# Cross attention and ternary FFN on one core: queries by tokens, four pairs of heads in flight, unrolled engine orders

## The chip, the cores and the metric

The kernel runs on one core of a Trainium2 chip. The metric is the device time of one execution in microseconds (us), lower is better. A core has five engines that take their instructions in order and meet only through semaphores: PE (matrix multiply; PEld is its weight load), DVE, ACT, POOL, and SP, which here only issues DMAs. The profile is a hardware trace of one execution.

## The reference, cut to what matters

```python
# x (4, 256, 256), ctx (4, 256, 128), 16 heads of 128, 1024 hidden
def xattn(h, ctx, Wq, Wk, Wv, Wo, gq, gk):
    q = rmsnorm((h @ Wq).reshape(B, Sq, H, D), gq)      # x * rsqrt(mean(x^2) + 1e-5) * g
    k = rmsnorm((ctx @ Wk).reshape(B, Skv, H, D), gk)
    v = (ctx @ Wv).reshape(B, Skv, H, D)
    attn = softmax(einsum('bqhd,bkhd->bhqk', q, k) / sqrt(D))
    return einsum('bhqk,bkhd->bqhd', attn, v).reshape(B, Sq, H * D) @ Wo
x = x + xattn(layernorm(x), ctx, ...)
w1, w2 = ternary(W_fc), ternary(W_proj)                 # groups of 64: round(w / mean|w|), times mean|w|
h = square(relu(layernorm(x) @ w1.T))
x = x + rms_norm(h) @ w2.T
```

## The kernel before, in words

The attention is done in 32 steps: 4 batches times 8 pairs of heads. One step takes one pair of heads of one batch through the whole chain, and the steps overlap. Matrices that need more than one fp32r pass are split into a high part (names with h at the end: qh, kh, PTh, Oh, Wqh) and a low part (ql, kl, PTl, Ol, Wql), and each product is three matmuls of 256 columns: `three` emits them at L547, L548 and L549. High parts are ACT copies out of PSUM, low parts DVE subtractions; Wqh, Wql, Wkh and Wkl are made by POOL from the raw loads. Wv is folded into Wo at the start (WWh, WWl), so attention multiplies the probabilities with the raw context (ch, cl) in bank bO, and project adds Oh and Ol times WW into bank bY.

Queries come out of PE transposed (bank bA, features on partitions). Their squares (qsq, ACT) are summed over the features by four matmuls against a column of ones (`sums_q`, L621), DVE adds the epsilon (qv), POOL takes the power -1/2 (fq, L297), and fq enters later, as the scale of the exponential and in the bias nb (DVE L918, maximum times fq). Keys come out by tokens (bank bB): ACT squares, DVE sums (L883), POOL takes the power (kv L291, rk L293), DVE multiplies (kn L887), and PE transposes kn. After exp (L416, accumulating the sums su) DVE takes the reciprocal rs; the probabilities of head 0 are normalised by POOL (L308), those of head 1 by ACT (L424). PE transposes them (L585).

The ternary weights of the FFN are prepared beside attention, a 32nd part in each step: ACT converts 2 groups (L429) and sums their absolute values (L433), DVE compares (L938, L939: wpos, wneg), POOL subtracts and scales (L314, L317, written into Wor's space).

The order on each engine is written out by hand in its `body(i)`, with hardware loops (Fori) over most steps. Each step has queries of pair i+1, keys of i+2, scores of i+1 and attention of i. After the steps comes the FFN (`up`, `down`, `square`, `hidden`), which the change leaves as it is, apart from the ramp into it.

Of the kernel before, what the change touches and what calls it, by code (L numbers as in the profile page):

```python
# [5 lines left out]
def xattn_ffn(nc, x, ctx, Wq, Wk, Wv, Wo, gq, gk, W_fc, W_proj, out):  # L6

# [18 lines left out]
    P = 128  # L26
# [17 lines left out]
    SG = NG // STEPS  # L44
# [10 lines left out]
    with es:  # L55
# [3 lines left out]
        def sem(name):  # L59
# [5 lines left out]
        Wqr = sb("Wqr", [P, KC, 2, D])  # L65
        Wkr = sb("Wkr", [P, 2, D])
# [4 lines left out]
        gg = sb("gg", [P, 1])  # L71
        fpr = sb("fpr", [P, NG, GROUP])
# [10 lines left out]
        xn = sb("xn", [P, NT, DIM])  # L83

# [12 lines left out]
        wabs = sb("wabs", [P, SG, GROUP], bf16)  # L97
        gsum = sb("gsum", [P, NG])
        gsr = sb("gsr", [P, SG], bf16)
        wpos = sb("wpos", [P, SG, GROUP], bf16)  # L100
        wneg = sb("wneg", [P, SG, GROUP], bf16)
# [40 lines left out]
        yo = xn  # L142

# [981 lines left out]
```

## Time and profile before

| | |
|---|---|
| runs | 370.31, 370.45, 375.02 us (median 370.45) |
| span of the profiled execution, first to last instruction | 373.6 us |
| time of the profiled execution around its span | not listed apart; its span is 3.15 us above the median of the runs |
| PE, PEld busy | 347.3 us (93%), 330.7 us (89%) |
| DVE, ACT, POOL busy | 308.3 us (83%), 295.5 us (79%), 256.4 us (69%) |
| granted TensorE clock, mean | 0.981 |

Read it by stage: the opening (0 to about 40 us), 32 steps that repeat (about 40 to 320 us), and the FFN (to 373.6 us). Matmuls overlap in the records: one of 256 columns lasts 0.28 us and the next starts 0.12 us later, so the cost of a matmul is the spacing of starts. The same holds for ACT and DVE, whose records overlap by some 0.1 us.

### The profile page before, as it was taken

The numbers are of one execution on the slowest core, as the hardware profiler recorded it, in microseconds if no ns is written. First come the engines' busy times: TensorE is split into PE (matmuls) and PEld (weight loads), VectorE is DVE, ScalarE is ACT, GpSimd is POOL, SyncE is SP. The second block draws the span as 40 slices with busy tenths as digits, with TensorE's granted clock in tenths as the row PEclk, the third lists the DMA queues.
The fourth block names the chain that finished last, engine by engine and source line by source line (L and its number), as shares of the span: only waits on it lengthen the run. The fifth ranks groups of instructions, "written<-read, shape, count | busy, mean of one in ns | idle before, by whom it ended". The sixth has DMA issues, their size and how long they took to land.

```text
span 373.6 us, 9069 instructions
## 1 busy us (share of the span) xinstructions
PE 347.3 (93%) x2720; PEld 330.7 (89%) x2720; DVE 308.3 (83%) x697; ACT 295.5 (79%) x810; POOL 256.4 (69%) x386
## 2 busy tenths in 40 slices
PE   6778999999999999999999999999999999888975
PEld 5768999999999999999999999999999998767865
DVE  2797788888888888888888898888888986799991
ACT  3447888888888888888888888888888888777750
POOL 3653777777777787777777877777778773065761
PEclk9989999999999999999999999999999999999995
DMA  6980111111111111111111111111111100000012
GB/s 212 366 281 6 55 42 42 42 42 42 44 44 42 42 42 45 42 42 44 42 44 43 42 43 42 44 42 44 45 51 53 51 1 0 2 0 2 0 38 75
DMA packets 20341, 20.72 MB, mean 55 GB/s; under 512 B 1504, under 2 KB 19936, under 8 KB 20192
## 3 DMA queue, kind: packets, MB, share of 16 engines
q1 hardware_dynamic: 20032, 20.45, 16.9%
q8 instruction: 12, 0.20, 0.2%
q14 instruction: 9, 0.07, 0.1%
q10 hardware_dynamic: 288, 0.00, 0.0%
HBM read 19.40 MB, written 1.05 MB: 55 GB/s over the span
## 4 chain that ended last, share of the span: by engine, by line
PE 48%; DVE 17%; POOL 13%; issue 12%; DMA 4%; ACT 3%; POOLq 1%; SPq 0%; DVEq 0%; ACTq 0%
POOL fq L297 7%; PE bY L547 6%; DVE WWl L869 4%; PE bT L585 4%; PE bY L549 4%; PE bY L548 4%; PE bA L547 3%; PE bA L548 3%; PE bA L549 3%; PE bT L595 3%; POOL Wkh L274 3%; DVE Ol L869 3%; DMA Wkr<-in_L_xattn_Wk 3%; PE bO L547 2%; PE bO L549 2%
## 5 line engine op out<-in xcount | busy, mean ns | idle before, releaser
L416 ACT ACTIVATE Pr<-bS,nb,fq 128x256 f32<-128x256 f32 x128 | 70.9, 564 | 1.7 <-DVE nb L918 1.7
L411 ACT ACTIVATE Oh<-bO 128x256 fp32r<-128x256 f32 x64 | 24.6, 385 | 29.5 <-PE bO L549 29.1
L277 POOL TENSOR_TENSOR Wql<-Wqr,Wqh 128x512 fp32r<-128x512 f32 x32 | 41.4, 1293 | 5.9 <-POOL Wqh L274 5.9
L914 DVE TENSOR_REDUCE mx<-bS 128x2 f32<-128x512 f32 x64 | 43.8, 684 | 1.0 <-PE bS L549 0.6
L547 PE MATMUL bY<-WWh,Oh 128*128 (+1 forms) x128 | 39.1, 305 | 5.8 <-DVE Ol L869 4.9
L869 DVE TENSOR_TENSOR PTl<-bT,PTh 128x512 fp32r<-128x512 f32 x64 | 43.5, 681 | 0.9 <-ACT PTh L403 0.5
L547 PE MATMUL bS<-kh,qh 128*128 128x256 f32 x128 | 41.5, 324 | 0.6 <-DVE kl L900 0.6
L869 DVE TENSOR_TENSOR ql<-bA,qh 128x512 fp32r<-128x512 f32 x32 | 22.1, 691 | 22.1 <-ACT qh L399 22.1
L403 ACT ACTIVATE PTh<-bT 128x512 fp32r<-128x512 f32 x64 | 38.0, 594 | 1.6
L585 PE MATMUL bT<-ident,Pr 128*128 128x128 f32 x256 | 38.4, 273 | 0.4 <-ACT Pr L424 0.4
L297 POOL TENSOR_TENSOR fq<-qv,mhalf 128x4 f32<-128x4 f32 x32 | 32.5, 1014 | 7.3 <-DVE qv L910 6.9
L274 POOL TENSOR_SCALAR Wkh<-Wkr 128x256 fp32r<-128x256 f32 x32 | 12.9, 404 | 35.6 <-PE bB L549 31.5
L547 PE MATMUL bO<-PTh,ch 128*128 128x256 f32 x128 | 36.3, 284 | 0.5 <-DVE PTl L869 0.5
L547 PE MATMUL bA<-xTh,Wqh 128*128 128x256 f32 x128 | 36.8, 287 | 0.0
L548 PE MATMUL bA<-xTl,Wqh 128*128 128x256 f32 x128 | 36.6, 286 | 0.0
L308 POOL TENSOR_SCALAR Pr<-Pr,rs 128x256 f32<-128x256 f32 x64 | 30.1, 481 | 9.3 <-DVE rs L923 6.3
L549 PE MATMUL bA<-xTh,Wql 128*128 128x256 f32 x128 | 36.3, 283 | 0.0
L549 PE MATMUL bS<-kh,ql 128*128 128x256 f32 x128 | 36.0, 281 | 0.0
L548 PE MATMUL bS<-kl,qh 128*128 128x256 f32 x128 | 36.0, 281 | 0.0
L549 PE MATMUL bO<-PTh,cl 128*128 128x256 f32 x128 | 35.9, 281 | 0.0
L549 PE MATMUL bY<-WWh,Ol 128*128 (+1 forms) x128 | 35.8, 279 | 0.0
L548 PE MATMUL bY<-WWl,Oh 128*128 (+1 forms) x128 | 35.8, 279 | 0.0
(172 smaller groups left out, 1293.0 us busy)
## 6 DMA issues: line engine op xcount, KB each, us to landing
Wqr<-in_L_xattn_Wq SPq DMA_DIRECT2D x32, 256.0 KB, 2.5
Wkr<-in_L_xattn_Wk SPq DMA_DIRECT2D x32, 128.0 KB, 2.4
Wor<-in_L_xattn_Wo SPq DMA_DIRECT2D x2, 1024.0 KB, 9.6
Wvr<-in_L_xattn_Wv SPq DMA_DIRECT2D x1, 1024.0 KB, 9.6
fpr<-in_L_ffn_W_fc SPq DMA_DIRECT2D x1, 1024.0 KB, 11.2
fpr<-in_L_ffn_W_proj SPq DMA_DIRECT2D x1, 1024.0 KB, 12.8
out<-xn SPq DMA_DIRECT2D x4, 256.0 KB, 2.2
xt<-in_x SPq DMA_DIRECT2D x1, 768.0 KB, 7.5
```

The source lines that it names most:

```text
L277: gp.tensor_tensor(lo, src, hi.bitcast(f32), ALU.subtract).then_inc(done, 1)
L297: gp.tensor_tensor(fq[:, :], qv[:, :], mhalf[:, 0:UT], ALU.pow).then_inc(fq_done, 1)
L308: last = gp.tensor_scalar(Pr[0][:, t, :], Pr[0][:, t, :], rs[0][:, t:t + 1], 1.0, ALU.mult, ALU.mult)
L403: act.activation(PTh[u][:, :, :].rearrange(flat3), bT[u][:, :], ACT.Copy).then_inc(pth_done[u], 1)
L411: act.activation(Oh[u][:, :], bO[:, u * SQ:(u + 1) * SQ], ACT.Copy).then_inc(oh_done, 1)
L416: last = act.activation(Pr[u][:, t, :], bS[u][:, t * SKV:(t + 1) * SKV], ACT.Exp, bias=nb[u][:, t:t + 1], scale=fq[:, QT * u + t:QT * u + ...
L547: pe.matmul(dst, sth, mvh, start=start, stop=False, **kw)
L548: pe.matmul(dst, sth, mvl, start=False, stop=False, **kw)
L549: return pe.matmul(dst, stl, mvh, start=False, stop=stop, **kw)
L585: last = pe.transpose(bT[u][:, k * SQ + t * P:k * SQ + (t + 1) * P], Pr[u][:, t, k * P:(k + 1) * P], ident[:, :])
L869: return dve.tensor_tensor(dst, src, hi.bitcast(f32), ALU.subtract)
L914: dve.tensor_reduce(mx[u][:, :], bS[u][:, :].rearrange("p (t k) -> p t k", t=QT), AX.X, ALU.max).then_inc(mx_done[u], 1)
```

## The change

Queries are now computed by tokens (x as the stationary operand, Wq moving), as keys were, with the same number of matmuls. ACT squares and accumulates the sums of the eight 128-column pieces of queries and keys directly out of PSUM (`square_q`, `square_k`: 8 instructions in place of 2). POOL's `norms` adds the epsilon and takes the power of all 8 columns in one call. DVE multiplies queries and keys out of PSUM (qn, kn), PE transposes both, and high and low parts are taken from the transposed banks (queries in bT0, keys in bT1, banks they share with the probabilities). `sums_q`, qv, fq, mx and DVE's sum of ksq are gone; the exponential has a constant scale, and nb is the negated maximum, written by one reduction. Both heads' probabilities are normalised by POOL. The ternary work goes in 8 chunks of 8 groups (128x512), one every third pass: the sums of absolute values are a DVE reduction (L948), no ACT instructions. Raw weights have two buffers. All loops are unrolled into one sequence on each engine, with queries of pair i+2, keys of i+2 (i+3 on ACT and POOL), scores of i+1, attention and projection of i-1 in PE's pass i. The opening, its banks (two instead of four for WW; one bank, bY, for the transposed x of batches 1 to 3) and the load order are new; semaphores are renamed.

The core of the diff:

```diff
-            def rsqrt_q(n):
-                gp.wait_ge(qv_done, n + 1)
-                gp.tensor_tensor(fq[:, :], qv[:, :], mhalf[:, 0:UT], ALU.pow).then_inc(fq_done, 1)
+            def norms(n):
+                gp.wait_ge(sqk_done, n + 1)
+                gp.wait_ge(sqq_done, n + 1)
+                gp.tensor_scalar(sse[:, :], ss[:, :], EPS * D, None, ALU.add).then_inc(sse_done, 1)
+                gp.wait_ge(sse_done, n + 1)
...
+                gp.tensor_tensor(rr[:, :], sse[:, :], mhalf[:, 0:2 * UT], ALU.pow).then_inc(r_done, 1)
...
+            for i in range(-2, STEPS):
+                if pair(i + 3):
                     split_k(i + 3)
...
+                if pair(i):
+                    norm_p(i, 1)
+                if pair(i + 2):
+                    norms(i + 2)
+                if pair(i + 3):
+                    split_q(i + 3)
+                if i == -1:
+                    ln_rstd(2, 1, B - 1)
+                if pair(i + 1):
+                    norm_p(i + 1, 0)
+                if i >= 4 and (i - 4) % 3 == 0 and (i - 4) // 3 < CHUNKS:
+                    ternary((i - 4) // 3)
...
+            def square_q(n):
                 act.wait_ge(q_done, n + 1)
-                act.activation(qsq[:, :, :].rearrange(flat3), bA[:, :], ACT.Square).then_inc(qsq_done, 1)
-                act.activation(qh[:, :, :].rearrange(flat3), bA[:, :], ACT.Copy).then_inc(qh_done, 1)
...
+                for j in range(UT):
+                    last = act.activation(sqj[:, j, :], bA[:, j * D:(j + 1) * D], ACT.Square,
+                                          accum_out=ss[:, j:j + 1])
+                last.then_inc(sqq_done, 1)
```

ACT's and PE's sequence after the change (the lines for the opening left out):

```python
for i in range(-2, STEPS + 1):              # ACT
    o_hi(i - 1, 1); square_q(i + 2); p_hi(i, 0); exps(i + 1, 0); p_hi(i, 1); exps(i + 1, 1)
    o_hi(i, 0); q_hi(i + 2); k_hi(i + 2); square_k(i + 3)
    if i >= 1 and (i - 1) % 3 == 0 and (i - 1) // 3 < CHUNKS:
        ternary((i - 1) // 3)
for i in range(-1, STEPS):                  # PE
    attend(i - 1, 0); turn_q(i + 1); keys(i + 2); turn_k(i + 1); queries(i + 2); attend(i - 1, 1)
    turn_p(i, 0); scores(i + 1, 0); scores(i + 1, 1); project(i - 1, 1); project(i - 1, 0); turn_p(i, 1)
for i in range(-3, STEPS):                  # DVE
    o_lo(i, 1); maxes(i + 2, 0); maxes(i + 2, 1); p_lo(i + 1, 0); q_norm(i + 3); k_norm(i + 3)
    recip(i + 2, 0); p_lo(i + 1, 1); o_lo(i + 1, 0); q_lo(i + 3); recip(i + 2, 1); k_lo(i + 3)
    if i >= 2 and (i - 2) % 3 == 0 and (i - 2) // 3 < CHUNKS:
        t_scale((i - 2) // 3)
    if i >= 3 and (i - 3) % 3 == 0 and (i - 3) // 3 < CHUNKS:
        t_compare((i - 3) // 3)
```

Two places in the order, before and after. The numbers behind names are banks and heads. **The ternary work and what stands behind it.** POOL before, one pass of its loop (the pass runs in a circle):

```order
L274 TENSOR_SCALAR Wkh<-Wkr 128x256
L277 TENSOR_TENSOR Wkl<-Wkr,Wkh 128x256
L297 TENSOR_TENSOR fq<-qv,mhalf 128x4
L274 TENSOR_SCALAR Wqh<-Wqr 128x512
L277 TENSOR_TENSOR Wql<-Wqr,Wqh 128x512
L291 TENSOR_SCALAR kv<-ssk 128x4
L293 TENSOR_TENSOR rk<-kv,mhalf 128x4
L308 TENSOR_SCALAR Pr0<-Pr0,rs0 128x256 x2
L314 TENSOR_TENSOR wpos<-wpos,wneg 128x128
L317 TENSOR_TENSOR Wor<-wpos,gsr 128x128
```

POOL now, from `norms(6)` in its pass i = 4 to `norms(7)` in pass 5:

```order
L327 TENSOR_SCALAR sse<-ss 128x8
L332 TENSOR_TENSOR rr<-sse,mhalf 128x8
L319 TENSOR_SCALAR Wqh<-Wqr1 128x512
L321 TENSOR_TENSOR Wql<-Wqr1,Wqh 128x512
L337 TENSOR_SCALAR Pr0<-Pr0,rs0 128x256 x2
L345 TENSOR_TENSOR wpos<-wpos,wneg 128x512
L347 TENSOR_TENSOR Wor<-wpos,gsr 128x512
L308 TENSOR_SCALAR Wkh<-Wkr0 128x256
L310 TENSOR_TENSOR Wkl<-Wkr0,Wkh 128x256
L337 TENSOR_SCALAR Pr1<-Pr1,rs1 128x256 x2
L327 TENSOR_SCALAR sse<-ss 128x8
L332 TENSOR_TENSOR rr<-sse,mhalf 128x8
```

The two separate powers became one of 8 columns, head 1's normalisation came in, and a ternary chunk of four times the size stands, in every third pass, ahead of the next norms. On DVE, before, a step from head 1's maxima to the keys' product:

```order
L914 TENSOR_REDUCE mx1<-bS1 128x2
L918 SCALAR_TENSOR_TENSOR nb1<-mx1,fq 128x2
L929 TENSOR_SCALAR gsr<-gsum 128x2
L923 RECIPROCAL rs0<-su0 128x2
L938 TENSOR_TENSOR wpos<-Wvr,gsr 128x128
L939 SCALAR_TENSOR_TENSOR wneg<-Wvr,gsr 128x128
L869 TENSOR_TENSOR Ol1<-bO,Oh1 128x256
L887 TENSOR_TENSOR kn<-bB,rk 128x512
```

DVE now, its pass i = 3, from the products of pair 6 to the first chunk's comparison:

```order
L907 TENSOR_TENSOR qn<-bA,rr 128x512
L913 TENSOR_TENSOR kn<-bB,rr 128x512
L935 RECIPROCAL rs0<-su0 128x2
L892 TENSOR_TENSOR PTl1<-bT1,PTh1 128x512
L892 TENSOR_TENSOR Ol0<-bO,Oh0 128x256
L892 TENSOR_TENSOR ql<-bT0,qh 128x512
L935 RECIPROCAL rs1<-su1 128x2
L922 SCALAR_TENSOR_TENSOR kl<-bT1,gg,kh 128x512
L958 TENSOR_TENSOR wpos<-Wvr,gsr 128x512
L959 SCALAR_TENSOR_TENSOR wneg<-Wvr,gsr 128x512
```

The comparison moved from among the waits for exp to behind the low part of the keys, which itself needs the transposed keys. **The squares.** ACT before, from Oh of head 1 into the next step:

```order
L411 ACTIVATE Oh1<-bO 128x256
L416 ACTIVATE Pr1,su1<-bS1,nb1,fq 128x256 x2
L490 REGISTER_ALU
L490 COMPARE_AND_BRANCH
L398 ACTIVATE qsq<-bA 128x512
```

ACT now:

```order
L410 ACTIVATE sqj,ss<-bB 128x128 x4
L452 ACTIVATE Oh1<-bO 128x256
L419 ACTIVATE sqj,ss<-bA 128x128 x4
L446 ACTIVATE PTh0<-bT0 128x512
L438 ACTIVATE Pr0,su0<-bS0,nb0 128x256 x2
```

The four accumulating squares of the queries stand directly behind Oh of head 1, the exponentials behind them.

## Rows read from the trace of the kernel before

**Rows 1.** Timeline of PE, one step: start, us, line, operation, out<-in, [idle before].

```profile
181.97 0.60 PE L585 MATMUL bT<-ident,Pr 128*128 128x128 f32 x4
...
182.53 0.28 PE L548 MATMUL bB<-Wkl,cTh 128*128 128x256 f32 x1
182.65 0.28 PE L549 MATMUL bB<-Wkh,cTl 128*128 128x256 f32 x1
...
183.12 0.95 PE L621 MATMUL bA<-ones,qsq 128*128 128x1 f32 x8
...
188.51 0.28 PE L549 MATMUL bO<-PTh,cl 128*128 128x256 f32 x1
```

**Rows 2.** Timeline of ACT, the same step.

```profile
182.17 0.69 ACT L407 ACTIVATE kh<-bT,gg 128x512 fp32r<-128x512 f32 x1
...
185.02 0.26 ACT L433 ACTIVATE wabs<-Wvr 128x64 bf16 x1
...
188.83 0.39 ACT L411 ACTIVATE Oh<-bO 128x256 fp32r<-128x256 f32 x1 [0.70 <-PE bO L549]
189.11 0.56 ACT L416 ACTIVATE Pr<-bS,nb,fq 128x256 f32<-128x256 f32 x1
```

**Rows 3.** Timeline of POOL: one row of the opening, then one step.

```profile
14.04 1.33 POOL L302 TENSOR_TENSOR rstd<-lnv,mhalf 128x6 f32<-128x6 f32 x1 [3.08 <-DVE lnv L854]
...
189.54 0.94 POOL L308 TENSOR_SCALAR Pr<-Pr,rs 128x256 f32<-128x256 f32 x2
190.44 0.43 POOL L314 TENSOR_TENSOR wpos<-wpos,wneg 128x128 bf16<-128x128 bf16 x1
191.05 0.40 POOL L317 TENSOR_TENSOR Wor<-wpos,gsr 128x128 bf16<-128x128 bf16 x1 [0.18 <-POOL wpos L314]
192.72 0.40 POOL L274 TENSOR_SCALAR Wkh<-Wkr 128x256 fp32r<-128x256 f32 x1 [1.27 <-PE bB L549]
...
194.01 1.01 POOL L297 TENSOR_TENSOR fq<-qv,mhalf 128x4 f32<-128x4 f32 x1
195.01 0.62 POOL L274 TENSOR_SCALAR Wqh<-Wqr 128x512 fp32r<-128x512 f32 x1
...
197.18 0.19 POOL L291 TENSOR_SCALAR kv<-ssk 128x4 f32<-128x4 f32 x1
197.46 1.02 POOL L293 TENSOR_TENSOR rk<-kv,mhalf 128x4 f32<-128x4 f32 x1
```

**Rows 4.** Timeline of DVE, the same step.

```profile
191.36 0.69 DVE L869 TENSOR_TENSOR ql<-bA,qh 128x512 fp32r<-128x512 f32 x1 [0.86 <-ACT qh L399]
192.11 0.75 DVE L900 SCALAR_TENSOR_TENSOR kl<-bT,gg,kh 128x512 fp32r<-128x512 f32 x1
192.78 0.68 DVE L869 TENSOR_TENSOR PTl<-bT,PTh 128x512 fp32r<-128x512 f32 x1
...
197.52 0.29 DVE L938 TENSOR_TENSOR wpos<-Wvr,gsr 128x128 bf16<-128x128 bf16 x1
```

**Rows 5.** Waits of the whole span: who waited for whom, us, times, longest.

```profile
DVE nb L918 <- POOL fq L297: 9.4, 26, 0.7
PEld bY L547 <- issue: 8.8, 20, 0.7
```

**Rows 6.** Timeline of PE, landmarks of the opening and the end.

```profile
7.07 1.97 PE L641 MATMUL bS<-ident,ct 128*128 128x128 f32 x8 [1.40 <-DMA ct<-in_ctx]
...
12.11 0.41 PE L548 MATMUL bA<-xTl,Wqh 128*128 128x256 f32 x1
...
12.32 0.41 PE L549 MATMUL bA<-xTh,Wql 128*128 128x256 f32 x1
...
48.83 0.28 PE L547 MATMUL bO<-PTh,ch 128*128 128x256 f32 x1
...
311.45 0.28 PE L547 MATMUL bO<-PTh,ch 128*128 128x256 f32 x1
...
319.89 0.38 PE L547 MATMUL bO<-PTh,ch 128*128 128x256 f32 x1 [0.51 <-DVE PTl L869]
```

More of the change, by code:

```diff
@@ L1 @@
+import math
 import concourse.bass as bass
@@ L632, in scores, with turn_p @@
                 last.then_inc(s_done[u], 1)
+            def turn_p(n, u):
+                pe.wait_ge(pn_done[u], n + 1)
+                ahead = min(n + 2, STEPS)
+                pe.wait_ge(kl_done if u else ql_done, ahead)
+                for t in range(QT):
+                    for k in range(KT):
+                        last = pe.transpose(bT[u][:, k * SQ + t * P:k * SQ + (t + 1) * P],
+                                            Pr[u][:, t, k * P:(k + 1) * P], ident[:, :])
+                last.then_inc(pt_done[u], 1)
@@ new lines, in attend @@
+            def attend(n, u):
+                b = n // PAIRS
+                pe.wait_ge(ptl_done[u], n + 1)
+                if u == 1:
+                    pe.wait_ge(ol_done[0], n + 1)
+                elif n >= 1:
+                    pe.wait_ge(ol_done[1], n)
+                for k in range(KT):
+                    last = three(bO[:, u * SQ:(u + 1) * SQ], ch[:, KT * b + k, :], cl[:, KT * b + k, :],
+                                 PTh[u][:, k, :], PTl[u][:, k, :], k == 0, k == KT - 1)
+                last.then_inc(av_done[u], 1)
@@ new lines, in project @@
+            def project(n, u):
+                b, p = divmod(n, PAIRS)
+                pe.wait_ge(ol_done[u], n + 1)
+                first = p == 0 and u == 1
+                if first and b:
+                    pe.wait_ge(x1_done, b)
+                if first and not b:
+                    pe.wait_ge(xl_done, B)
+                if b == 0:
+                    pe.wait_ge(wwl_done, p + 1)
+                for t in range(QT):
+                    s = slice(t * P, (t + 1) * P)
+                    last = three(bY[:, t * DIM:(t + 1) * DIM], Oh[u][:, s], Ol[u][:, s],
+                                 WWh[:, 2 * p + u, :], WWl[:, 2 * p + u, :],
+                                 first and t == 0, False, skip_group_check=True)
+                last.then_inc(y_done, 1)
@@ new lines, in turn_wv, with wv_wo @@
+            def turn_wv(n):
+                if n >= 2:
+                    pe.wait_ge(ctl_done, n - 1)
+                for t in range(4):
+                    last = pe.transpose(wv_banks[n][:, t * P:(t + 1) * P], Wvr[:, 4 * n + t, :], ident[:, :])
+                last.then_inc(wv_turned, 1)
+            def wv_wo(n):
+                if n % 4 == 0:
+                    pe.wait_ge(s_wo[n // 4], 16)
+                if n == 0:
+                    pe.wait_ge(wvt_done, 4)
+                if n >= 2:
+                    pe.wait_ge(wwl_done, n - 1)
+                for t in range(2):
+                    last = pe.matmul(ww_banks[n % 2][:, t * DIM:(t + 1) * DIM], WvT[:, 2 * n + t, :],
+                                     Wor[:, 2 * n + t, :], start=True, stop=True)
+                last.then_inc(ww_done, 1)
@@ L638, in _ @@
             pe.wait_ge(s_c, 16)
[L639 to L648 removed]
+            turn_ctx(0)
+            turn_ctx(1)
```

1021 lines of the change are left out of this document (486 added, 535 removed).

## The prediction

> **What bounds the kernel now.** I read the shares first (PE busy 93%, the others 69% to 83%), then one step on each timeline, then the waits. PE starts attention of pair 1 at 48.83 and of pair 30 at 311.45 [rows 6]: 29 steps in 262.62 us, 9.06 us each. A step holds 54 matmuls of 256 columns whose starts lie 0.118 us apart (rounded to 0.12 in [rows 1]), 6.37 us; three blocks of four transposes, of which one with its switch back costs 181.97 to 182.53 less one matmul, 0.44 us; and the eight sums of the squares, 0.88 (their record of 0.95 less the overlap with what follows) [rows 1]. That is 8.57 us of PE work; the other 0.5 us are waits. PE is nearly the bound, but not alone: the nb of every step waits for POOL's power (9.4 us in 26 waits), and loops cost PE issue gaps (8.8 us in 20) [rows 5].
>
> **PE's own work, and loops.** The sums go (-0.88 us), transposing queries comes (+0.44): 8.13 us a step, and with nothing else in the way 0.93 us a step less. The issue gaps of [rows 5] stand where a loop computes an address; unrolling gives back at most 8.8/32 = 0.3 us a step, all inside the 0.5 us of waits above. The Trainium skill (Runtime: NRT & Kernel Launch, section Instruction fetch mechanics) says that a taken branch out of the fetched window forces a fetch stall and that kernels therefore prefer full unrolling; by it alone the change gains. The trace bounds that gain by the 0.3 us, and I book none beyond PE's sum, since another chain ends last now.
>
> **The new chain through all engines.** PE cannot start the keys of pair n+1 before DVE has taken those of n out of bank bB (`keys` waits on kn_done), and POOL's `norms(n)` now makes both factors only after the four squares of the queries, which ACT does behind Oh of head 1, the output of the attention that PE runs right behind these queries. One turn, from the end of queries to the end of the next queries:
> - attention of head 1, 6 matmuls: 0.71; PE to ACT 0.20 (last start 188.51 plus its 0.12 slot, ACT at 188.83) [rows 1, 2]
> - Oh 0.28 (188.83 to 189.11) [rows 2]
> - four accumulating squares of 128 columns. No such row exists. The bounds are 0.26 (64 columns) and 0.56 (256 columns) [rows 2]; the line between them gives 0.36 at 128. I take 0.32 from start to start, a little less, since the next operation starts before a record ends (Oh's is 0.39 long, Pr starts 0.28 behind it), and 0.10 for the last to end: 4 x 0.32 + 0.10 = 1.38
> - to POOL 0.08; sse 0.28 (197.18 to 197.46); the power of 8 columns: 4 columns take 1.02 and 6 take 1.33, so 1.64 [rows 3]. Lower bound 1.33, upper 2 x 1.02
> - to DVE 0.10; qn and kn, 0.60 to the next start and 0.69 to the end (as ql, PTl [rows 4]); to PE 0.06
> - keys 0.71, transposed keys 0.44, queries 1.42 [rows 1]
>
> Sum 8.59 us. It is longer than PE's 8.13, so a plain step takes 8.6 us, 0.46 less than now. ACT (sum of its starts about 7.1 us) and DVE (about 6 us) fit beside it. POOL needs norms 2.0, split of Wq 2.17 (195.01 to 197.18), head 0's and head 1's normalisation 0.90 each, split of Wk 1.29 [rows 3]: 7.3 us, which fits too. For the bounds: squares at 0.26 and a power of 1.33 give 8.1, squares at 0.54 give 9.5.
>
> **The passes with a ternary chunk.** In every third pass, eight times, POOL's queue holds `ternary(c)` between head 0's normalisation and the split of Wk, head 1's normalisation and the next `norms` (the order rows above). It waits for DVE's comparison of the same chunk. That stands behind kl of the pair whose norms POOL made in this same pass, and kl needs PE's transposed keys. So POOL goes idle after some 5 us of work, and everything queued behind it, the norms that start the next turn among them, waits. From `norms(6)` to `norms(7)`:
> - norms 1.92, to DVE 0.10, qn and kn 1.29, to PE 0.06, keys 0.71, transposed keys 0.44, to ACT 0.20, kh 0.69, to DVE 0.04, kl 0.67 to the next start (192.11 to 192.78 [rows 4]): 6.12
> - two comparisons of 512 columns: 128 columns take 0.29 [rows 4]. Bounds 0.29 and four times that; I take 0.60 and 0.70, about the cost of other 512-column operations there: 1.30; to POOL 0.08
> - POOL's two operations on 512 columns: at 128 they take 0.43 and 0.40 with 0.18 between. From 256 to 512 columns a split costs 0.88 more (194.01 - 192.72 = 1.29 for Wk, 197.18 - 195.01 = 2.17 for Wq), of which 0.22 is its first operation (0.40 to 0.62) and 0.66 its subtraction [rows 3]. For 384 more columns that is 0.33 and 0.99; the chunk's two operations have two full operands like the subtraction, but in bf16, and I take 0.75 for each: 1.18 + 0.18 + 1.15 = 2.5. Bounds 1.0 and 3.5
> - 0.05, split of Wk 1.29, head 1's normalisation 0.90, hop 0.10: 2.34
>
> Sum 12.3 us, 3.7 more than a plain turn. Since the plain turn is a closed chain, nothing catches up later. With the shortest price of every unknown (power 1.33, comparisons and POOL's pair at their 128-column rows) it is still 9.8 us. ACT's share of the chunk falls in passes that POOL delays anyway: nothing. Removed ternary work on ACT (0.26 each for the absolute values [rows 2]) frees an engine that does not bind.
>
> **Residual.** At three batch ends DVE adds the residual between kn and PTl, which the transposed keys wait for: 3 x 0.6 = 1.8 us.
>
> **The opening.** The context is turned at 7.07 to 9.04 [rows 6] as before. Then, by the same prices and with PE at its slower spacing (12.11 to 12.32, 0.21 [rows 6]): layer norm stands behind the context's low parts, x is turned by 12.8, queries of pair 0 end at 16.9. Squares, norms, qn and kn take until 22, queries of pair 1 until 26. Scores, the first exponentials and WW in two banks hold qn of pair 1 until 32; queries of pair 2 end at 36. The last four WW products alternate with scores until 41, DVE subtracts and normalises the other three batches until 45, and only then come maxima, PTl and qn of pair 2: attention of pair 0 at 47. Turning batches 1 to 3 through the one bank bY costs two round trips of PE, ACT, DVE and PE, 2.9 and 2.4 us. Attention of pair 1 starts at 60, 11 us later than at 48.83. I give this 56 to 64.
>
> **The end.** The old trace takes 8.44 us from attention of pair 30 to that of 31 (311.45 to 319.89 [rows 6]); with the scores of 31 already done the new order has 7.0 us there. From 311.45 to the end of the span, 373.6, are 62.15 us; now 60.65.
>
> **The sum.** 60 + 21 x 8.6 + 8 x 12.3 + 1.8 + 60.65 = 401.5 us of span. The profiled span of before, 373.6, lies 3.15 above the median of the runs, 370.45, and I take the same off: 398 us.
>
> **Rivals.**
> 1. The ternary chunk is hidden: POOL does not stand still, because DVE reaches the comparison some 2.5 us sooner than I place it. Against it: the rows of the order have kl before it without exception. Then 60 + 29 x 8.6 + 1.8 + 60.65 = 371.9, less 3.15 = 369 us, no change that a measurement tells.
> 2. The change does what a deeper pipeline should: all factors arrive in time, PE alone is the bound at 8.13, the opening ends where it did. 48.8 + 29 x 8.13 + 60.65 = 345, 342 us. This is the side on which the kernel gets faster; it needs squares and power together at least 0.5 us cheaper than my rows, and the chunks hidden. For it speaks only that POOL, ACT and DVE each have room in their sums.
> 3. Accumulating squares cost what the exponentials do (0.54 from start to start): a plain turn is 9.5, and 60 + 21 x 9.5 + 8 x 12.3 + 1.8 + 60.65 = 420.4, 417 us.
> 4. The chunk waits, but its operations cost little more than at 128 columns: 60 + 21 x 8.3 + 8 x 9.8 + 1.8 + 60.65 = 375, 372 us; between here and my forecast lies every price in between.
>
> **How the numbers follow.** A measurement of this kernel tells about 2% (7.4 us) from no change. Forecast 0.70 (384 to 411 us by the bounds of turn, chunk and opening), case 4 and what lies up to 384: 0.06, rival 1: 0.10, rival 2: 0.06, rival 3: 0.08. The range 372 to 414 leaves out rivals 1 and 2 and the worse half of 3. Above 377.9 lie the forecast, rival 3 and over half of case 4: 0.81; below 363 rival 2 and a little of rival 1: 0.08; the rest, 0.11, is within 2%.
>
> **What would show it.** In the new trace: POOL's wpos (L345) waits for DVE's wneg some 2.5 us in each of eight passes, the power (L332) takes about 1.64, `norms` recur every 8.6 us and every third time 12.3 between passes 4 and 26, squares follow at 0.32, attention of pair 1 starts near 60. PE's idle time grows to some 3.7 us per chunk, ended by Pr of head 1 or by qn. I am wrong if L345 does not wait, or if the plain turn is not set by keys waiting for kn.

## The result, and the profile after

The changed kernel takes 421.23 us (median of four runs, 418.7 to 424.46) against 372.45 us of the kernel before in the same comparison: a ratio of 1.133, 95% interval 1.123 to 1.143. It is slower, as forecast, but by more than the range held (398, range 372 to 414). The profiled execution took 418.7 us with a span of 416.9 us, against 373.6 us of span before.

The page of the changed kernel, its busy times:

```profile
PE 353.3 (85%) x2592; PEld 329.6 (79%) x2592; DVE 281.6 (68%) x537; ACT 267.9 (64%) x1042; POOL 267.9 (64%) x370
```

and two rows of its 40 slices, PE's busy tenths and the granted clock:

```profile
PE   5679579996996977996997897996996998888984
...
PEclk9999889999998998998898999899998799999996
```

No engine is the bound any more: PE stood at 93% before and is at 85%. The busy row dips every third or fourth slice all through the loop, and the clock dips beside it. Both have the rhythm of the ternary chunks.

The same landmarks of PE as in [rows 6], the attention of pairs 0, 1, 30 and 31, in the changed kernel's timeline:

```profile
47.69 0.58 PE L559 MATMUL bO<-PTh,ch 128*128 128x256 f32 x1 [2.43 <-DVE PTl L892]
...
63.09 0.37 PE L559 MATMUL bO<-PTh,ch 128*128 128x256 f32 x1
...
356.64 0.36 PE L559 MATMUL bO<-PTh,ch 128*128 128x256 f32 x1
...
363.65 0.37 PE L559 MATMUL bO<-PTh,ch 128*128 128x256 f32 x1
```

So the opening is 14.3 us longer (63.09 against 48.83), the loop from pair 1 to pair 30 is 30.9 us longer (293.55 against 262.62), and the end is 1.9 us shorter (60.26 against 62.15): 43.3 us in all.

The waits of the whole span (who waited for whom, us, times, longest), which answer to [rows 5]:

```profile
POOL sse L327 <- ACT sqj L419: 60.0, 22, 8.3
DVE qn L907 <- POOL rr L332: 51.4, 30, 6.4
...
POOL wpos L345 <- DVE wneg L959: 21.6, 8, 3.1
...
POOL rstd L302 <- DVE lnv L882: 20.3, 3, 14.1
...
PEld bB L559 <- issue: 5.2, 22, 0.2
```

The first two belong to the closed chain of a turn, in which POOL waits for squares and then DVE for POOL. They are the longest rows, and the forecast has them inside its turns. The third is the forecast wait for the comparison, eight times 2.7 us. The fourth was in nobody's sum: its longest, 14.1 us, is at the end, where the kernel before waits in the same way (10.37 us, at 329.56); the other two, 3.46 and 2.72 us, are in the loop.

POOL's timeline with the first chunk and the turn behind it answers to [rows 3]:

```profile
87.77 0.25 POOL L327 TENSOR_SCALAR sse<-ss 128x8 f32<-128x8 f32 x1 [1.48 <-ACT sqj L419]
88.10 1.66 POOL L332 TENSOR_TENSOR rr<-sse,mhalf 128x8 f32<-128x8 f32 x1
...
91.82 0.94 POOL L337 TENSOR_SCALAR Pr<-Pr,rs 128x256 f32<-128x256 f32 x2
95.39 1.16 POOL L345 TENSOR_TENSOR wpos<-wpos,wneg 128x512 bf16<-128x512 bf16 x1 [2.63 <-DVE wneg L959]
96.62 1.04 POOL L347 TENSOR_TENSOR Wor<-wpos,gsr 128x512 bf16<-128x512 bf16 x1
...
99.84 0.24 POOL L327 TENSOR_SCALAR sse<-ss 128x8 f32<-128x8 f32 x1
...
109.53 0.25 POOL L327 TENSOR_SCALAR sse<-ss 128x8 f32<-128x8 f32 x1 [2.22 <-ACT sqj L419]
```

The reader is to see three things: the power of 8 columns at 1.66 us, the 2.63 us in which POOL stands before wpos, and the distances of `norms` (L327): 12.07 us from 87.77 to 99.84, and then 9.69 us to 109.53 in a turn that holds no chunk. The page's windows show what is different in that one (stretch, its length and PE busy, granted clock, DMA share, GB/s):

```profile
99.84:109.53 9.69, 8.26 (x58) 0.82 0.19 55
109.53:118.11 8.58, 8.55 (x73) 1.00 0.15 48
```

PE runs the turn behind the chunk at a granted clock of 0.82, the mean of a stretch at the lower of its two levels (1.2 GHz) and the rest at the upper (2.4 GHz). In PE's timeline there, the keys' matmuls start 0.21 us apart instead of 0.12, behind two long idle stretches:

```profile
99.81 0.66 PE L635 MATMUL bT<-ident,Pr 128*128 128x128 f32 x4 [1.78 <-POOL Pr L337]
...
102.61 1.11 PE L605 MATMUL bT<-ident,qn 128*128 128x128 f32 x4 [1.44 <-DVE qn L907]
...
103.74 0.41 PE L560 MATMUL bB<-Wkl,cTh 128*128 128x256 f32 x1
103.95 0.41 PE L561 MATMUL bB<-Wkh,cTl 128*128 128x256 f32 x1
```

The squares on ACT, of which the kernel before had no row, and in the same kernel the layer norm of a finished batch on POOL:

```profile
95.05 0.27 ACT L419 ACTIVATE sqj<-bA 128x128 bf16<-128x128 f32 x1
...
95.30 0.28 ACT L419 ACTIVATE sqj<-bA 128x128 bf16<-128x128 f32 x1
...
148.57 0.71 POOL L302 TENSOR_TENSOR rstd<-lnv,mhalf 128x2 f32<-128x2 f32 x1 [3.46 <-DVE lnv L882]
```

The squares lie 0.25 us apart, each with its accumulator read inside that. The power of the layer norm waits 3.46 us for DVE exactly as a ternary chunk does: it stands in POOL's queue ahead of head 1's normalisation and the next `norms`, and DVE makes lnv only behind kl.

### The profile page after: what moved, and what is told of

The parts are those of the page before. It is cut to its first block, busy times and chain, and to the rows that moved or that the text cites. A ratio compares the mean times of both kernels' runs of the same rounds, so it can differ in the third digit from the quotient of the medians.

```text
span 416.9 us, 8120 instructions
## 1 busy us (share of the span) xinstructions
PE 353.3 (85%) x2592; PEld 329.6 (79%) x2592; DVE 281.6 (68%) x537; ACT 267.9 (64%) x1042; POOL 267.9 (64%) x370
## 3 DMA queue, kind: packets, MB, share of 16 engines
q1 hardware_dynamic: 20032, 20.45, 15.4%
## 4 chain that ended last, share of the span: by engine, by line
PE 50%; POOL 17%; DVE 16%; issue 8%; ACT 6%; DMA 1%; POOLq 0%; DVEq 0%; SPq 0%; ACTq 0%
POOL rr L332 6%; PE bT L605 5%; PE bT L614 4%; PE bT L635 3%; DVE WWl L892 3%; PE bB L559 3%; PE bA L559 3%; PE bA L560 3%; PE bA L561 3%; POOL Pr L337 3%; PE bO L559 2%; POOL wpos L345 2%; PE bO L561 2%; PE bO L560 2%; POOL Wor L347 2%
## 5 line engine op out<-in xcount | busy, mean ns | idle before, releaser
L337 POOL TENSOR_SCALAR Pr<-Pr,rs 128x256 f32<-128x256 f32 x128 | 59.9, 480 | 8.1 <-DVE rs L935 8.0
L438 ACT ACTIVATE Pr<-bS,nb 128x256 f32<-128x256 f32 x128 | 59.4, 472 | 6.2 <-DVE nb L928 6.2
L332 POOL TENSOR_TENSOR rr<-sse,mhalf 128x8 f32<-128x8 f32 x32 | 53.2, 1663 | 2.9 <-POOL sse L327 0.4
L635 PE MATMUL bT<-ident,Pr 128*128 128x128 f32 x256 | 39.5, 278 | 14.8 <-POOL Pr L337 14.8
L928 DVE TENSOR_REDUCE nb<-bS 128x2 f32<-128x512 f32 x64 | 43.6, 689 | 9.1 <-PE bS L561 8.4
L327 POOL TENSOR_SCALAR sse<-ss 128x8 f32<-128x8 f32 x32 | 8.2, 255 | 60.8 <-ACT sqj L419 60.0
L892 DVE TENSOR_TENSOR PTl<-bT,PTh 128x512 fp32r<-128x512 f32 x64 | 43.3, 676 | 3.4 <-ACT PTh L446 3.4
L635 PEld LDWEIGHTS bT<-ident,Pr 128*128 128x128 f32 x256 | 29.4, 141 | 17.1 <-POOL Pr L337 16.9
L559 PE MATMUL bA<-Wqh,xTh 128*128 128x256 f32 x128 | 41.5, 324 | 1.5 <-DVE xTl L892 1.5
L892 DVE TENSOR_TENSOR Ol<-bO,Oh 128x256 fp32r<-128x256 f32 x64 | 26.9, 421 | 17.3 <-ACT Oh L452 17.2
L560 PE MATMUL bA<-Wql,xTh 128*128 128x256 f32 x128 | 38.3, 299 | 0.0
L561 PE MATMUL bA<-Wqh,xTl 128*128 128x256 f32 x128 | 38.1, 298 | 0.0
L559 PE MATMUL bY<-WWh,Oh 128*128 128x256 f32 x128 | 36.5, 285 | 1.5 <-DVE Ol L892 1.5
L560 PE MATMUL bO<-PTl,ch 128*128 128x256 f32 x128 | 37.0, 289 | 0.0
```

Of the source, the lines that this page charges most:

```text
L332: gp.tensor_tensor(rr[:, :], sse[:, :], mhalf[:, 0:2 * UT], ALU.pow).then_inc(r_done, 1)
L337: last = gp.tensor_scalar(Pr[u][:, t, :], Pr[u][:, t, :], rs[u][:, t:t + 1], 1.0, ALU.mult, ALU.mult)
L438: last = act.activation(Pr[u][:, t, :], bS[u][:, t * SKV:(t + 1) * SKV], ACT.Exp, bias=nb[u][:, t:t + 1], scale=1.0, accum_out=su[u][:, t: ...
L559: pe.matmul(dst, sth, mvh, start=start, stop=False, **kw)
L560: pe.matmul(dst, sth, mvl, start=False, stop=False, **kw)
L561: return pe.matmul(dst, stl, mvh, start=False, stop=stop, **kw)
```

## The experiments

All are changes of the changed kernel. Each was compared with the kernel before, which ran beside it. The loop is from attention of pair 1 to that of pair 30, as above.

| kernel | span | pair 1 at | loop | end | ratio to before, 95% interval |
|---|---|---|---|---|---|
| before | 373.6 | 48.83 | 262.6 | 62.2 | |
| the change | 416.9 | 63.09 | 293.6 | 60.3 | 1.133 (1.123 to 1.143) |
| e1_later | 391.0 | 64.94 | 263.7 | 62.3 | 1.044 (1.039 to 1.049) |
| e2_halves | 376.6 | 63.07 | 251.3 | 62.2 | 1.014 (1.008 to 1.020) |
| e3_filler | 436.8 | 64.75 | 308.4 | 63.7 | 1.172 (1.165 to 1.178) |
| e4_powers | 381.8 | 62.83 | 256.6 | 62.3 | 1.024 (1.019 to 1.028) |
| e5_filler2 | 410.6 | 62.90 | 284.0 | 63.7 | 1.100 (1.093 to 1.107) |
| e6_opening | 371.2 | 58.05 | 250.9 | 62.3 | 0.999 (0.993 to 1.005) |
| e7_dve | 372.9 | 64.05 | 245.0 | 63.9 | 1.000 (0.992 to 1.007) |
| e8_all | 364.4 | 58.05 | 244.1 | 62.3 | 0.982 (0.976 to 0.988) |
| e9_act | 362.2 | 58.09 | 241.7 | 62.4 | 0.970 (0.964 to 0.977) |
| e10_port | 370.5 | 57.66 | 250.5 | 62.3 | 1.002 (0.997 to 1.007) |

### e1_later: the chunk one pass later on POOL

```diff
-                if i >= 4 and (i - 4) % 3 == 0 and (i - 4) // 3 < CHUNKS:
-                    ternary((i - 4) // 3)
+                if i >= 5 and (i - 5) % 3 == 0 and (i - 5) // 3 < CHUNKS:
+                    ternary((i - 5) // 3)
```

> The changed kernel with one edit: POOL's ternary(c) stands one pass later (the same place in its pass), so that DVE's comparison is long done when POOL comes to it. Theory A (POOL's queue waits for the comparison, and everything behind it with it): the wait before wpos (L345, 21.6 us in eight times) is gone. POOL's own work in a pass with a chunk is then 7.1 + 2.25 = 9.4 us, so such a turn takes 9.4 instead of 12.09. With PE never long idle, the turns behind chunks, 9.7 to 11.4 now at a granted clock of 0.69 to 0.84, come back to 8.6. The three layer norms between batches, whose power on POOL waits for DVE in the same way, stay as they are, 1 to 3 us each. Loop (attention of pair 1 to that of pair 30) 293.6 - 8 x 2.7 - 12 = 260 us, span about 383. Rival B (what a chunk costs is the work that it brings to DVE, POOL and ACT, not where it stands): no turn gets below 11, span 410 or more.

Measured: the wait before wpos is gone from the list. Seven of the eight turns in which POOL holds the chunk take 9.43 to 9.46 us for a forecast of 9.4, the eighth 10.47 with a layer norm beside it, and the two other turns with a layer norm 11.35 and 11.70. Nearly all the rest take 8.57 to 8.60, those behind chunks too. The loop is 263.7 us, 29.8 less than in the changed kernel; the span fell less than forecast (391 against 383), since 3.7 us of the miss are the loop and the rest lies in the opening (1.9) and the end (2.1), where the granted clock was lower than in the changed kernel (0.66 against 0.83 from 45 to 65 us, 0.90 against 0.94 behind attention of pair 30). The same instructions in the same numbers, one pass later: theory A stands, rival B falls.

### e2_halves: no pass of POOL with a whole chunk, and the layer norm's power later

```diff
-                    ternary((i - 4) // 3)
+                if i >= 5 and (i - 5) % 3 == 0 and (i - 5) // 3 < CHUNKS:
+                    ternary_dif((i - 5) // 3)
+                if i >= 6 and (i - 6) % 3 == 0 and (i - 6) // 3 < CHUNKS:
+                    ternary_mul((i - 6) // 3)
-                if i >= PAIRS and i % PAIRS == 1:
+                if i >= PAIRS and i % PAIRS == 2:
                     ln_rstd(2 + i // PAIRS, i // PAIRS - 1)
```

> As the run before, and besides POOL's two operations of a chunk stand in two different passes (the subtraction one pass later than in the changed kernel, the product two), and the power of the layer norms between batches one pass later. No pass of POOL then holds more than 7.1 + 1.2 = 8.3 us. Theory A: every turn is the plain one of 8.58 us, with some 0.6 more at batch ends for the residual: loop 29 x 8.58 + 1.5 = 250 us, span 63.1 + 250.3 + 60.3 = 374, within 1% of the kernel before (373.6). If chunks cost by their work on DVE (2.5 us in three passes) instead of by the wait, turns with DVE's part of a chunk stay above 9 and the span is over 385.

Measured: 20 of the 27 turns from `norms(4)` on take 8.55 to 8.60 us, with DVE's part of the chunks in them; those with a residual take 9.08 or 9.09 (three times), those with a layer norm 8.85 to 8.99. The loop is 251.3 us. So the whole slowdown of the loop was the place of two things in POOL's queue, and with them out of the way the turn is the plain one that was forecast, 0.48 us shorter than the 9.06 of before. What is left against the kernel before is the opening.

### e3_filler and e5_filler2: what the clock costs

The first of these put its matmuls into the wrong pass, one before the idle time, where they stood in the chain of the turn. This is its edit; e5_filler2 has 5 in place of 4 and 6 in place of 5.

```diff
+            def filler(dst, count):
+                for _ in range(count):
+                    pe.matmul(dst[:, 0:DIM], WWh[:, 0, 0:P], WWl[:, 0, :], start=True, stop=True)
...
                     attend(i - 1, 0)
+                if i >= 5 and (i - 5) % 3 == 0 and (i - 5) // 3 < CHUNKS:
+                    filler(bT[0], 12)
...
                     project(i - 1, 0)
+                if i >= 4 and (i - 4) % 3 == 0 and (i - 4) // 3 < CHUNKS:
+                    filler(bO, 14)
```

> The changed kernel, with matmuls that no one reads put into PE's two idle stretches around each ternary chunk: 14 behind the projection in the pass with the chunk (into bO), 12 behind the next attention of head 0 (into bT0), each about as long as the wait it stands in (1.8 and 1.44 us at 0.12 a matmul). Nothing that a chunk waits for is changed. Theory C (the turn behind a chunk takes 9.7 to 11 us instead of 8.6 because PE runs it at a granted clock of 0.69 to 0.84 after its idle time): the clock stays at 1.00 there, turns with a chunk stay at 12.1, turns behind one fall to 8.6 to 8.8, span 416.9 - 11 = 406. Rival D (the turn behind a chunk is long because ACT and DVE have a backlog from the wait, the clock only goes with it): the clock stays up, but the turns behind chunks stay at 9.7 and more, span 416 to 418.

Measured: seven of the eight turns with a chunk grew from 12.1 to 14.8 us (15.47 with a layer norm beside it), with POOL waiting 5.3 us instead of 2.63 before wpos; the eighth (12.17) stands behind a layer norm. So 3.1 us of PE work inside the turn lengthen it by 2.7: the turn is a closed chain through PE, with little slack. The idle stretches were not filled, so this is not the test that was meant, but its turns behind a chunk can be sorted by their clock. In three of them it was 1.00, behind idle stretches of up to 1.80 and 1.44 us all the same, and they took 8.53, 8.58 and 9.10 us (the last with a residual). Four without a layer norm ran at 0.67, 0.68, 0.80 and 0.82 and took 10.31, 10.62, 8.66 and 9.60. That already speaks for the clock, and it shows that the same idle time does not bring the clock down each time.

> The run e3_filler repeated with the matmuls one pass later, where PE really stands idle: 14 ahead of the transposes of head 1's probabilities that wait for POOL behind a chunk (1.8 us), 12 ahead of the next transposes of the queries (1.44 us). Theory C (the clock makes the turn behind a chunk long): turns with a chunk stay at 12.1, turns behind one fall from 9.7 to 11 to about 8.6, and the clock of those stretches rises from 0.69 to 0.84 to nearly 1.00: span 416.9 - 11 = 406. Rival D (a backlog on ACT and DVE): the clock rises, the turns behind chunks stay, span 416.

Measured, windows of the turn with the first chunk, the one behind it and a plain one (cut at the starts of `norms` less 0.2 us):

```profile
87.39:99.49 12.10, 12.07 (x100) 1.00 0.07 23
99.49:108.06 8.57, 8.41 (x69) 1.00 0.22 64
108.06:116.63 8.57, 8.53 (x72) 1.00 0.15 46
```

The turns with a chunk stay at 12.1 us and the wait before wpos at 21.6 us, to the digit. The turns behind them, of the changed kernel 9.69, 9.91, 8.67, 10.86, 10.62, 9.91, 9.99 and 11.05, are now 8.57 where they hold nothing else (six of eight; the second has a residual, 9.08, the fifth a layer norm, 10.47), and the clock there is 1.00. The loop is 9.6 us shorter. Theory C stands and rival D falls: the backlog was no cause. How much a turn loses depends on where the slow stretch lies: the third turn of the changed kernel ran at a mean of 0.80 and still took only 8.67 us, since its clock was low already at its start (four transposes at 163.55 took 1.00 us instead of 0.66) and PE's second idle stretch shrank to 0.52 us. Of the 9.6 us, the span shows only 6.3, because the end ran 3.5 us longer than in the changed kernel (its granted clock behind attention of pair 31 was 0.87 against 0.93); its program is unedited. The Trainium skill (TensorE: Matmul & The Clock Gate, section HAM oscillation) describes a kernel in which the waits between its bursts of matmuls put the engine back to half rate, over and over; the trace agrees, with 0.21 us from start to start behind the gaps and 0.12 without them.

### e4_powers and e7_dve: what a plain turn hangs on

e4_powers is e2_halves with `norms` in two calls:

```diff
+            def norms_k(n):
+                gp.wait_ge(sqk_done, n + 1)
+                gp.tensor_scalar(sse[:, UT:2 * UT], ss[:, UT:2 * UT], EPS * D, None, ALU.add).then_inc(ssk_done, 1)
...
+                gp.tensor_tensor(rr[:, UT:2 * UT], sse[:, UT:2 * UT], mhalf[:, 0:UT], ALU.pow).then_inc(rk_done, 1)
...
-                gp.tensor_tensor(rr[:, :], sse[:, :], mhalf[:, 0:2 * UT], ALU.pow).then_inc(r_done, 1)
+                gp.tensor_tensor(rr[:, 0:UT], sse[:, 0:UT], mhalf[:, 0:UT], ALU.pow).then_inc(r_done, 1)
```

> As e2_halves, and POOL's norms is made in two calls: epsilon and power of the four key columns as soon as ACT's key squares are there, and only the four query columns behind the query squares. The power behind the query squares then takes 1.02 instead of 1.66 us. Theory E (a plain turn is the closed chain attention of head 1, Oh, squares, norms, qn and kn, keys, transposed keys, queries): the chain falls by 0.64 to 7.95, below PE's 8.13, so a turn takes about 8.15: span 374 - 29 x 0.43 = 361. Rival F (a plain turn is set by something else, POOL's sum above all, which rises to 7.9 plus gaps here, or DVE): 8.58 stays or grows, span 374 or more.

Measured: the distances of the query norms are 7.91, 8.13 and 8.18 us up to the first chunk, and then 8.85 to 9.08 for nearly all of the loop. Theory E holds for the first three, rival F for the rest. The shortened chain does bring the turn to PE's 8.13. But two powers of 4 columns take 1.04 each where one of 8 took 1.66, POOL's work rises to 7.8 us, and with half a chunk (1.1) it is full. Every third turn holds no part of a chunk on POOL, and yet six of these eight take 8.85 to 8.89 us: there DVE compares, and head 1's normalisation on POOL takes 1.89 to 1.93 us instead of 0.94 (first row below). The last experiment is about that. POOL of e4_powers, that row, and then one pass with half a chunk, without a single idle time:

```profile
91.34 1.93 POOL L345 TENSOR_SCALAR Pr<-Pr,rs 128x256 f32<-128x256 f32 x2
...
108.07 1.04 POOL L357 TENSOR_TENSOR Wor<-wpos,gsr 128x512 bf16<-128x512 bf16 x1
...
110.28 0.94 POOL L345 TENSOR_SCALAR Pr<-Pr,rs 128x256 f32<-128x256 f32 x2
111.30 0.23 POOL L328 TENSOR_SCALAR sse<-ss 128x4 f32<-128x4 f32 x1
111.61 1.04 POOL L332 TENSOR_TENSOR rr<-sse,mhalf 128x4 f32<-128x4 f32 x1
112.64 0.24 POOL L336 TENSOR_SCALAR sse<-ss 128x4 f32<-128x4 f32 x1
112.96 1.04 POOL L340 TENSOR_TENSOR rr<-sse,mhalf 128x4 f32<-128x4 f32 x1
```

e7_dve takes the chunk from POOL altogether:

```diff
+            def t_finish(c):
+                dve.wait_ge(t_pn, c + 1)
+                dve.tensor_tensor(wpos[:, :, :], wpos[:, :, :], wneg[:, :, :], ALU.subtract).then_inc(t_dif, 1)
+                dve.wait_ge(t_dif, c + 1)
+                dve.tensor_tensor(wt[:, CG * c:CG * (c + 1), :], wpos[:, :, :], ..., ALU.mult).then_inc(t_done, 1)
...
+                if i >= 4 and (i - 4) % 3 == 0 and (i - 4) // 3 < CHUNKS:
+                    t_finish((i - 4) // 3)
```

> As e4_powers, and both of POOL's operations of a ternary chunk are done by DVE, at the end of its pass behind the comparison. In e4_powers a turn took 7.9 to 8.2 us before the first chunk and 8.9 from there on, with POOL never idle. Theory G (there POOL's sum was the bound, and the shortened chain is right): POOL has 7.8 us left, PE 8.13, DVE 6.1 + 1.2 on the mean: a turn takes 8.15 to 8.3 throughout, span 63 + 29 x 8.2 + 1.5 + 60 = 362. Rival H (DVE's order holds a turn once it has 3.8 us more in three passes): turns of 8.6 and more in each pass with DVE's part of a chunk, span 372 or more.

Measured: turns of 8.9, 8.4 and 7.9 us in rotation (with DVE's comparison, with its product, with neither). The loop is 245.0 us, 11.6 less than e4_powers, against a forecast of 8.2 a turn or 239. The turn with the comparison did not fall, though POOL no longer has the chunk. Neither theory holds as written: G has no turn of 8.9, and H has all turns with DVE's part of a chunk at 8.6 or more, where those with its product take 8.4. POOL has no idle time in most turns, and its normalisation of head 1 takes 1.9 us beside the comparison; the last experiment is about that.

### e6_opening and e8_all: the opening

```diff
-        x1_banks = [bT[0], bY, bY, bY]
+        x1_banks = [bT[0], bY, bO, bY]
...
                     for n in range(4, PAIRS):
+                        if n - 3 < B:
+                            ln_norm(n - 3, 2)
                         ww_lo(n)
-                    for b in range(1, B):
-                        ln_norm(b, 2)
...
                 if i == 0:
                     turn_x1(1)
+                    turn_x1(2)
```

with ACT's and DVE's copies of batches 1 and 2 moved ahead of p_hi and p_lo of pair 0.

> As e2_halves (span 376.6, attention of pair 1 at 63.1), with another opening: the x of batches 1 to 3 is normalised between the low parts of WW instead of behind them, batch 2's x is turned in bank bO at the same time as batch 1's in bY and both are copied ahead of the first p_hi, and only batch 3's is turned in pass 1. If the opening is lost on the single bank's round trips and on DVE's normalisations in a row, attention of pair 1 starts about 7 us sooner (2.0 of the normalisations, 5 of the round trips at half clock), at 56, and the span is 370. If ACT's and DVE's own order in the opening holds it, it stays within 2 us of 63 and the span within 2 of 376.6.

Measured: pair 1's attention starts at 58.05 us instead of 63.07, and the span is 371.2, 5.4 us less. The forecast was 7. The single bank and the normalisations in a row cost 5.0 us together; some 9 us against the kernel before are left, and 8.4 of them lie ahead of attention of pair 0, which comes at 47.88 here, at 47.69 in the changed kernel and at 39.47 in the kernel before. I did not take those apart.

> e7_dve with the opening of e6_opening. The gains add up if the opening and the loop are separate: span 355 when both hold (e7's 362 less 7). This is the version meant to beat the kernel before, 373.6.

Measured: span 364.4, 8.5 less than e7_dve, and 0.982 of the kernel before (0.976 to 0.988). The gains add: of the 8.5 us, 6.0 lie ahead of attention of pair 1, 0.9 in the loop and 1.6 in the end. Of the 9 us above the forecast of 355, 4.8 are the loop, whose turns with DVE's parts of a chunk stay at 8.4 and 8.9, 2 the opening and 2.3 the end.

### e9_act: less for POOL

```diff
+            def norm_a(n):
+                act.wait_ge(rec_done[1], n + 1)
+                act.activation(Pr[1][:, 1, :], Pr[1][:, 1, :], ACT.Copy, scale=rs[1][:, 1:2]).then_inc(pa_done, 1)
...
                     k_hi(i + 2)
+                if pair(i + 1):
+                    norm_a(i + 1)
```

and on POOL, in `norm_p(n, u)`:

```diff
-                for t in range(QT):
+                for t in range(QT - u):
```

> e8_all, and ACT normalises the second query tile of head 1's probabilities, behind the high part of the keys, in POOL's place (0.47 us less for POOL, 0.5 more for ACT, which stands idle some 1.5 us a turn there). In e8_all turns take 8.88, 8.37 and 7.9 us by turns (chunk compared, chunk finished, no chunk) and POOL hardly ever waits. If POOL's sum sets the first two, they fall to 8.4 and 8.15 and the span by 29 x 0.16 = 5 us to 359 or 360. If ACT's longer way to Oh of head 1 counts (the key squares stand behind the new instruction, Oh and the query squares behind those), nothing is gained: 364 to 367.

Measured: 0.970 of the kernel before (0.964 to 0.977), the fastest version of this study, with a loop of 241.7 us, 2.3 less than e8_all, and a span 2.2 us less. Most turns with a comparison take 8.6 to 8.85, those with the product some 8.2. In the former POOL now stands idle 0.75 to 0.94 us (but for one with a layer norm), so its sum no longer sets them; what does was not tested. The gain is half of the forecast, and the interval touches that of e8_all, so that it is the version of the two by its span, not clearly by its ratio.

### e10_port: POOL and DVE side by side

Where POOL no longer waits for the comparison, from e1_later on, it works on head 1's normalisation while DVE compares. POOL's and DVE's timelines in e8_all:

```profile
86.03 1.93 POOL L345 TENSOR_SCALAR Pr<-Pr,rs 128x256 f32<-128x256 f32 x2
...
86.41 0.68 DVE L960 TENSOR_TENSOR wpos<-Wvr,gsr 128x512 bf16<-128x512 bf16 x1
87.01 0.69 DVE L961 SCALAR_TENSOR_TENSOR wneg<-Wvr,gsr 128x512 bf16<-128x512 bf16 x1
```

The two instructions, which take 0.94 us in most turns, take 1.93. It is so in seven of the eight passes with a comparison in e8_all (1.88 to 1.95), and likewise in six or seven each of e1_later, e2_halves and e4_powers, but never in the changed kernel, where POOL stands idle while DVE compares. The experiment moves the comparison:

```diff
                     residual(i // PAIRS)
+                if i >= 4 and (i - 4) % 3 == 0 and (i - 4) // 3 < CHUNKS:
+                    t_compare((i - 4) // 3)
                 if pair(i + 2):
                     recip(i + 2, 0)
...
-                if i >= 3 and (i - 3) % 3 == 0 and (i - 3) // 3 < CHUNKS:
-                    t_compare((i - 3) // 3)
```

> e8_all, with DVE's comparison of a chunk moved from the end of its pass to behind kn of the next pass. In e8_all POOL's normalisation of head 1 (two instructions, 0.94 us) takes 1.9 us in the eight passes in which DVE compares beside it. Theory P (POOL stands still while DVE runs an operation whose operands all lie in SBUF): the stretch moves with the comparison: the normalisation of head 1 is back at 0.94, and the split of Wq (0.62 + 1.28), which POOL does then, takes about 1.2 longer in the same eight passes; turns with a comparison stay near 8.9, span 364. Rival Q (the normalisation was long for another reason, a late semaphore or its own operands): 0.94 again and the split unchanged, turns 8.2, span 359.

Measured, POOL and then DVE in the same stretch:

```profile
90.41 1.29 POOL L323 TENSOR_TENSOR Wql<-Wqr,Wqh 128x512 fp32r<-128x512 f32 x1
93.03 0.94 POOL L345 TENSOR_SCALAR Pr<-Pr,rs 128x256 f32<-128x256 f32 x2 [1.33 <-DVE rs L937]
...
91.03 1.22 DVE L960 TENSOR_TENSOR wpos<-Wvr,gsr 128x512 bf16<-128x512 bf16 x1
92.17 0.68 DVE L961 SCALAR_TENSOR_TENSOR wneg<-Wvr,gsr 128x512 bf16<-128x512 bf16 x1
92.77 0.15 DVE L937 RECIPROCAL rs<-su 128x2 f32<-128x2 f32 x1
```

Head 1's normalisation is back at 0.94 us beside the comparison's old place, which both theories had. The split of Wq did not grow, against what I wrote for theory P. It was DVE that stood still: wpos takes 1.22 us instead of 0.68, and its end lies 0.55 us behind the end of POOL's subtraction (91.70). The same distance comes back in the turns in which wpos starts at another point of the split: it takes 1.38 us from 143.33, with the subtraction ending at 144.17, and only 0.68 from 117.60, where a residual ahead of it put it behind all but 0.13 us of the subtraction. So the two engines exclude each other, as theory P has it, but whichever comes second waits; in e8_all that was POOL, here it is DVE. This reading was made after the run, which was not forecast so; the other runs named above agree with it. Q's turn of 8.2 us falls too: 9.7 was measured, since the reciprocal behind the comparison came 1.3 us late. The Trainium skill (SBUF — State Buffer, section SBUF: two separate sides) says that the two share a pair of ports, which goes to whichever starts first for its whole instruction, a DVE operation with two inputs in SBUF or a POOL operation that reads SBUF, while the other waits; both traces agree, by 0.99 us on POOL in e8_all and 0.54 us on DVE here.

## Why the prediction was right and wrong

The forecast had the direction, the main mechanism (POOL's wait for the comparison) and its size, and missed the time by 23 us. Of these, 15.4 are in the span (401.5 worked out, 416.9 measured); the rest lies in how a span stands to the median: I took 3.15 us off, the profiled execution lay 1.8 us above its span, and the median 2.5 us above that execution. I had set the profiled span of the kernel before, which was that of the longest of its three runs (375.02 us), against their median, 370.45.

- **The plain turn, 8.59 us:** measured 8.58. The parts were nearly as sized (squares 0.25 apart for 0.32, power 1.66 for 1.64), and the small differences cancel. That it is a closed chain through POOL's norms is shown by e4_powers, where a power shorter by 0.6 us brings the turn to 8.13 us, PE's own sum, as long as POOL has room.
- **The turn with a chunk, 12.3 us:** measured 12.06 to 12.22 in six of eight (12.60 and 12.77 with a residual or a layer norm beside it). The wait before wpos is 2.63 us for a forecast of some 2.5, its two operations 2.25 for 2.5. That the wait is the cause and not the work is shown by e1_later.
- **"Nothing catches up later", taken as the end of it:** this is the step that failed, a chunk's after-effect put at nothing. I priced the turn behind a chunk as a plain one. PE had stood idle 1.78 and 1.44 us just before, and runs part of it at the lower clock: 9.6 us over the loop, shown by e5_filler2. The clock before was 1.00 all through the loop, but 0.93 from 20 to 45 us, and the slower spacing stood in my own rows of the opening (0.21 us, [rows 6]); with 3.7 us of new idle time per chunk in the forecast, it had to be priced.
- **The residual, 1.8 us at three batch ends:** measured 0.5 each. What I left out of the same batch ends is larger: the power of the layer norm stands in POOL's queue in the same way as the chunk and waits for DVE behind kl. It costs 2.80, 1.90 and 0.68 us where it stands (turns of e5_filler2, which has it without the clock, against its neighbours), 5.4 us; the first two with a wait, the third, right behind a chunk, only by its own length. The trace before had this power too (0.71 us at 136.96, 209.47 and 281.98), but without a wait in the loop. I looked for waits of the chunk, not for every entry of POOL's queue that waits for DVE.
- Together: 9.6 + 5.4, less 1.6 for the chunks, 0.4 for the plain turns and 0.3 for the residual, is 12.7 of the 12.75 us by which the loop was longer than forecast.
- **The opening, 60 us:** measured 63.09. Attention of pair 0 came at 47.69 for 47, so 2.4 us of the miss are in the 15.4 us behind it. PE ran them at a granted clock of 0.78, but the forecast had priced the opening at the slower spacing already, so the clock is not what it left out. That the single bank and the normalisations are worth 5.0 us is shown by e6_opening; which term of the opening was too small stays open. At a clock of 0.62 to 0.64 the same stretch took 16.9 to 17.0 us (e1_later, e3_filler, e7_dve).
- **The end, 60.65 us:** measured 60.26. The gain of the order is there: attention of pair 31 comes 7.01 us behind that of pair 30, for a forecast of 7.0 and 8.44 before, and 7.0 in every experiment. But seven of the ten experiments, with the same end, took 62.2 to 62.4 us from pair 30 on and three 63.7 to 63.9, for 62.15 in the kernel before. Behind pair 31 they need 55.2 to 56.9 us, where the kernel before needs 53.71 and the changed one 53.25. The clock explains this in part (0.93 in the changed kernel, 0.86 to 0.90 in the experiments), but the kernel before had 0.90 too; the rest stays open. So the forecast of the whole end was met with some luck.
- **PE alone at 8.13 and unrolling:** the issue wait that came back in most steps is smaller, 0.2 us in each of 22 times (5.2 us) for 0.4 to 0.7 in 20 (8.8 us). Single ones of up to 2.5 us in the opening and at the end bring all issue waits of PEld to 17.2 us, for 11.6 before. No run shows a gain from unrolling by itself, and none was booked.

Of the rivals, the third (squares like exponentials, 417 us) was nearest in time and wrong in cause: the squares took 0.25 us, not 0.54.

## What to carry to other kernels

Walk the queue of the engine that starts the next turn, and for every entry that waits for another engine ask where that engine makes it. An entry that is rare and unimportant holds all that stands behind it, and moving it by one pass gave back 26 us of 417 here without changing an instruction, the clock behind it included. When a forecast contains a new idle stretch of PE, price the work behind it at the slower spacing of matmuls too. A shorter chain helps until the next sum is full: with the power cut in two, POOL's work decided, and only together with less work on POOL and a shorter opening did the new order beat the old one (0.982, then 0.970). When a wait is taken away, look at what then runs side by side: POOL's normalisation met DVE's comparison only after POOL had stopped waiting for it.

## What the runs showed of the hardware that was not expected

- POOL and DVE exclude each other for whole instructions when both work in SBUF: 1.93 us instead of 0.94 for two instructions of POOL beside a comparison of DVE, and 1.22 instead of 0.68 for the comparison when POOL was first. Operations of DVE that read PSUM (kl, ql, PTl) ran beside POOL's without a change of either. DVE's subtraction and product of a chunk also lengthen what POOL does beside them: an epsilon from 0.24 to 0.54 us in e8_all, a power from 1.04 to 1.46 in e10_port.
- An accumulating ACT pass of 128 columns out of PSUM costs 0.25 us from start to start, its accumulator read included, no more than the record of one operation on 64 columns, 0.26 us [rows 2].
- POOL's power grows slowly with its columns (4: 1.04, 8: 1.66 us), so cutting it in two shortens the chain but costs 0.4 us more in sum, and the second epsilon.
